# GpSimd adds the states of two pairs, and the order of all engines moves with it: residual and last attention group ahead of the convolution, whose second half uses another PSUM bank

## The reference

```
L0  whitening over 4 channel groups (means and a 4x4 covariance over all images), then a 4x4 mix and a bias
L1  per image: LayerNorm over channels, W_in -> xi, z (256 channels each); causal 4-tap convolution of xi, silu -> xc
    W_x: xc -> dt (8), B (16), C (16);  delta = softplus(W_dt dt + b)
    for n in 16 states:  h = h * exp(delta * A_n) + delta * xc * B_n      (a scan over the 1024 positions)
    y = sum_n h * C_n + xc * Dp;   y = y * silu(z);   out = W_out y + residual
L2  attention over the 1024 positions of an image (q, k, v, softmax), times gamma, plus its input
L3  a second attention (theta, phi, values = x), a 1x1 convolution, BatchNorm over all images, plus its input
```

## Time and profile before

| | |
|---|---|
| median of 3 runs | 5972.65 us (5970.45 to 5973.8) |
| profiled execution | 5973.68 us, its span 5971.9 us |
| PE busy | 5277.8 us (88%) |
| DVE busy | 5084.5 us (85%) |
| POOL busy | 3913.3 us (66%) |
| ACT busy | 3698.7 us (62%) |
| first scan, last scan start | 188.1 us, 5716.8 us |
| one round in the middle (copy into psU of k = 0 to the next one) | 2930.05 to 3106.84 us |

### The profile page before, as it was taken

One profiled execution on the slowest core, in us unless ns is written; L12 is line 12 of the kernel. 1 busy time (PEld: TensorE's weight loads), 2 busy tenths in 40 slices (PEclk: granted clock), 3 DMA queues, 4 the chain that ended last, 5 costly groups with the idle time before them and its releaser, 6 DMA issues.

```text
span 5971.9 us, 63803 instructions
## 1 busy us (share of the span) xinstructions
PE 5277.8 (88%) x18611; PEld 2975.7 (50%) x18611; DVE 5084.5 (85%) x5978; ACT 3698.7 (62%) x6077; POOL 3913.3 (66%) x2702
## 2 busy tenths in 40 slices
PE   6689999999999999999999999999999999999971
PEld 6245555545555555555555455555545555554541
DVE  5799888988988898988889888888888989888843
ACT  2566666666666666666666666666666666666643
POOL 0677766667766776767677776666766767767620
PEclk9799999999999999999999999999999999999996
DMA  3565555555555555555555555555555555555527
GB/s 125 204 229 206 206 206 198 207 207 205 207 207 205 204 210 205 211 201 212 205 196 211 213 205 201 205 207 196 211 212 204 208 205 207 202 205 212 199 106 285
DMA packets 199104, 1216.99 MB, mean 204 GB/s; under 512 B 27880, under 2 KB 28656, under 8 KB 67696
## 3 DMA queue, kind: packets, MB, share of 16 engines
q1 hardware_dynamic: 194416, 1196.26, 54.4%
q10 hardware_dynamic: 4352, 16.78, 0.7%
HBM read 1158.43 MB, written 54.53 MB: 203 GB/s over the span
## 4 chain that ended last, share of the span: by engine, by line
PE 38%; DVE 27%; ACT 19%; issue 13%; DMA 1%; POOL 1%; DVEq 1%; SPq 0%; ACTq 0%; POOLq 0%
PE psE L812 13%; PE psA L812 11%; DVE hs L486 11%; DVE psD L482 10%; PE psT L812 6%; ACT da L678 5%; ACT p L724 4%; PE psT L984 4%; DVE nm L511 3%; ACT pt L688 3%; PE psY L812 2%; ACT L647 1%; ACT L749 1%; ACT sz L650 1%; PE psD L812 1%
## 5 line engine op out<-in xcount | busy, mean ns | idle before, releaser
L301 POOL TENSOR_TENSOR pa<-hs,rows_all 128x1024 f32<-128x1024 f32 x1024 | 2410.4, 2354 | 1580.5 <-DVE hs L486 1577.8
L482 DVE TENSOR_TENSOR psD<-rows_all,psU 128x512 f32<-128x512 f32 x2048 | 1416.3, 692 | 70.2 <-POOL hlast L305 1.2
L678 ACT ACTIVATE da<-delta,neg_a 128x512 f32<-128x512 f32 x2048 | 1367.7, 717 | 119.4 <-DVE hs L486 108.7
L486 DVE TENSOR_TENSOR_SCAN hs<-da,hlast,psD 128x512 f32<-128x512 f32 x1024 | 1310.9, 1280 | 36.3
L486 DVE TENSOR_TENSOR_SCAN hs<-da,psD 128x512 f32<-128x512 f32 x1024 | 1248.9, 1220 | 36.1 <-ACT da L678 0.9
L812 PE MATMUL psY<-pa,ident 128*128 128x512 f32 x2304 | 1184.8, 610 | 50.7 <-POOL pa L308 30.5
L308 POOL TENSOR_TENSOR pa<-pa 128x512 f32<-128x512 f32 x896 | 1137.5, 1270 | 35.1
L724 ACT ACTIVATE p<-psE,nm 128x1024 f32<-128x1024 f32 x512 | 569.6, 1112 | 710.2 <-DVE nm L511 710.2
L812 PE MATMUL psA<-pt,va 128*128 128x256 f32 x4096 | 976.0, 387 | 2.6 <-DVE x L529 1.6
L812 PEld LDWEIGHTS psA<-pt,va 128*128 128x128 f32 x4096 | 794.8, 196 | 250.4 <-issue 153.9
L688 ACT ACTIVATE pt<-psT 128x512 f32<-128x512 f32 x1024 | 560.6, 597 | 451.6 <-PE psT L984 445.2
(11 more groups left out here) (180 smaller groups left out, 4564.7 us busy)
## 6 DMA issues: line engine op xcount, KB each, us to landing
rows_all<-bc_scratch SPq DMA_DIRECT2D x1024, 1024.0 KB, 4.7
xin<-x SPq DMA_DIRECT2D x40, 512.0 KB, 5.7
xres<-x SPq DMA_DIRECT2D x64, 256.0 KB, 4.2
x_scratch<-x SPq DMA_DIRECT2D x32, 512.0 KB, 2.9
f_scratch<-fa SPq DMA_DIRECT2D x32, 512.0 KB, 3.2
xres<-x SPq DMA_DIRECT2D x8, 512.0 KB, 3.2
x1g<-x SPq DMA_DIRECT2D x8, 512.0 KB, 3.3
fa<-x SPq DMA_DIRECT2D x8, 512.0 KB, 3.2
```

The costliest lines, as they stand in the source:

```text
L301: pool.tensor_tensor(pa[:, k % PROD, :, :], hs[:, sl, :, :], rows_all[:, slot, 2:4, :], ALU.mult).then_inc(S["prod"], 1)
L482: dve.tensor_tensor(psD[:, :], rows_all[:, slot, j, :], psU[:, :], ALU.mult).then_inc(S["dbu_ok"], 1)
L486: dve.tensor_tensor_scan(hs[:, sl, j, :], da[:, sl, j, :], psD[:, :], hlast[:, h, n_:n_ + 1] if ch else 0.0, ALU.mult, ALU.add).then_inc(S ...
L678: act.activation(da[:, k % 2, j, :], delta[:, h, cols(ch)], ACT.Exp, scale=neg_a[:, h, 2 * q + j:2 * q + j + 1]).then_inc(S["da_ok"], 1)
```

## The change

**GpSimd.** Every step now adds its two states (also 14 and 15), and every odd step then adds the slots of the two steps into one ("quad"). PE sums one slot for two steps: 8 matmuls a half. `prod`, `pair` and `quad` count POOL's stages; a slot comes free when PE has summed the quad (`quad_mm`).

**Order.** On PE the residual moves from line 3 to line 2, "weigh0 weigh1" of the last group stays in line 3, and the convolution follows: "inner0" from line 2 to 4, "inner1" from line 4 to 6. `normed` moves from step 2 to 3, the convolution's evictions on ACT from steps 3, 5 to 5, 7. Tile 1 is turned at step 10 (was 9); the groups are weighed one line later except the last, and `attended` moves from 12, 15 to 13, 16. "rows" moves ahead of the energy of tile 2, "steps" behind that of tile 3.

**Bank.** "inner1" goes to psA in place of psT's second bank and waits for the last attended group (`out_ok`); "project" waits only for the first half's eviction.

```
-ADDED = [r for r in range(16) if r not in (14, 15)]
...
-        TURN_AT = [8, 9, 12, 12, 14, 15, 17, 18]
+        TURN_AT = [8, 10, 12, 12, 14, 15, 17, 18]
...
-        WEIGH_AT = [(11, 11), (13, 14), (16, 17), (19, 19)]
-        ATTEND_AT = [12, 15, 18, 20]
+        WEIGH_AT = [(11, 12), (14, 15), (17, 18), (19, 19)]
+        ATTEND_AT = [13, 16, 18, 20]
...
-        AT_C, AT_N, AT_X, AT_Z, AT_B, AT_P = 0, 2, (3, 5), 9, 10, 11
+        AT_C, AT_N, AT_X, AT_Z, AT_B, AT_P = 0, 3, (5, 7), 9, 10, 11
...
-                    wait(pool, "pair_mm", b, k - PROD + 1)
+                    wait(pool, "quad_mm", b, k // 2 - 1)
...
-                    if k % NS in ADDED:
-                        wait(pool, "prod", b, k + 1)
...
+                    wait(pool, "prod", b, k + 1)
+                    pool.tensor_tensor(pa[:, k % PROD, 0, :], pa[:, k % PROD, 0, :], pa[:, k % PROD, 1, :], ALU.add
+                                       ).then_inc(S["pair"], 1)
+                    if k % 2:
+                        wait(pool, "pair", b, k + 1)
+                        pool.tensor_tensor(pa[:, k % PROD, 0, :], pa[:, (k - 1) % PROD, 0, :], pa[:, k % PROD, 0, :], ALU.add
+                                           ).then_inc(S["quad"], 1)
...
-                        act.activation(xc[:, h, cols(fc)], psT[:, h, :], ACT.Identity, bias=cbias[:, h, 0:1]
+                        act.activation(xc[:, h, cols(fc)], (psT[:, 0, :], psA[:, :])[h], ACT.Identity, bias=cbias[:, h, 0:1]
...
-                            wait(pe, "pt_ok", *att["turned1"])
+                            wait(pe, "pt_ok", *att["turned0"])
...
+                        dst = (psT[:, 0, :], psA[:, :])[h]
+                        if beside and h == 0:
                             wait(pe, "pt_ok", *beside["turned7"])
+                        if beside and h == 1:
+                            wait(pe, "out_ok", *beside["attended3"])
...
+                    if k % 2 == 0:
+                        return
+                    wait(pe, "quad", b, (k + 1) // 2)
+                    mm(psY[:, :], ident[:, :], pa[:, k % PROD, 0, :], start=(q == 1), stop=(q == PAIRS - 1)
+                       ).then_inc(S["quad_mm"], 1)
...
+                    if t == 1 and front:
+                        wait(pe, "z_ok", front[0], 2 * front[1] + 2)
...
-                    "turn add inner0",
-                    "weigh0 weigh1 residual add",
...
+                    "weigh1 turn add residual",
+                    "weigh0 weigh1 add",
```

More of the change, by code:

```diff
@@ L181, in build @@
             u_ok=2 * NCH, dbu_ok=2 * STEPS, da_ok=2 * STEPS, h_ok=2 * STEPS,
-            hlast_ok=STEPS // 2, prod=STEPS, added=NCH * len(ADDED), pair_mm=STEPS, g_ok=2 * NCH,
+            hlast_ok=STEPS // 2, prod=STEPS, pair=STEPS, quad=STEPS // 2, quad_mm=STEPS // 2, g_ok=2 * NCH,
             x1_mm=NCH, x1_ok=NCH, x1g_ok=NCH,
@@ L490, in gate @@
                 def gate(b, ch, h):
-                    wait(dve, "pair_mm", b, NS * ch + PAIRS * (h + 1))
+                    wait(dve, "quad_mm", b, (NS * ch + PAIRS * (h + 1)) // 2)
                     dve.tensor_tensor(g[:, h, cols(ch)], psY[:, :], sz[:, h, cols(ch)], ALU.mult
@@ L638, in front @@
                         h = AT_X.index(r)
-                        wait(act, "pair_mm", fb - 1, NS * (fc + 1))
+                        wait(act, "quad_mm", fb - 1, NS // 2 * (fc + 1))
                         wait(act, "xi_mm", fb, 2 * fc + h + 1)
-                        act.activation(xc[:, h, cols(fc)], psT[:, h, :], ACT.Identity, bias=cbias[:, h, 0:1]
+                        act.activation(xc[:, h, cols(fc)], (psT[:, 0, :], psA[:, :])[h], ACT.Identity, bias=cbias[:, h, 0:1]
                                        ).then_inc(S["xi_ok"], 1)
@@ L745, in image @@
                                 key(b - 1, c)
-                            if front_of and r == AT_X[1]:
+                            if front_of and r == AT_X[0]:
                                 front(*front_of, r)
@@ L757, in image @@
                                 value(b - 1, c)
-                            if front_of and r not in (AT_X[1], AT_Z):
+                            if front_of and r not in (AT_X[0], AT_Z):
                                 front(*front_of, r)
@@ L896, in front @@
                         wait(pe, "z_ok", fb, 2 * fc + 2)
+                        if att:
+                            wait(pe, "pt_ok", *att["turned1"])
                         for h in range(NH):
@@ L916, in front @@
                         wait(pe, "xc_ok", fb, 2 * fc + 2)
-                        if beside:
-                            wait(pe, "out_ok", *beside["attended3"])
+                        wait(pe, "xi_ok", fb, 2 * fc + 2)
                         for h in range(NH):
@@ L926, in sum_states @@
                     group, q = divmod(k, PAIRS)
-                    if q == 0:
+                    if q == 1:
                         wait(pe, "g_ok", b, group)
[L929 to L938, removed]
+                    if k % 2 == 0:
[3 more added lines that the diff above has]
+                       ).then_inc(S["quad_mm"], 1)
                 def skip_term(b, ch, h):
@@ L1016, in project @@
                     if front:
-                        wait(pe, "xi_ok", front[0], 2 * front[1] + 2)
-                    elif beside:
+                        wait(pe, "xi_ok", front[0], 2 * front[1] + 1)
+                    if beside:
                         wait(pe, "pt_ok", *beside["turned7"])
@@ L1033, in _ @@
                 ORDER = [
-                    "centre energy add weigh0 variance",
-                    "energy weigh1 turn add",
-                    "turn add inner0",
-                    "weigh0 weigh1 residual add",
-                    "inner1 add",
+                    "centre energy add variance",
+                    "energy turn add weigh0",
+                    "weigh1 turn add residual",
+                    "weigh0 weigh1 add",
+                    "inner0 add",
                     "project add",
-                    "add project_values",
+                    "project_values add inner1",
                     "energy add",
                     "energy turn add skip0",
[L1043 to L1049, removed]
+                    "gates add rows",
+                    "energy turn add",
+                    "energy steps add weigh0",
+                    "turn weigh1 turn_more skip1 add",
+                    "energy add",
+                    "energy turn weigh0 add",
+                    "turn weigh1 add",
                 ]
```

9 lines of the change are left out of this document (3 added, 6 removed).

## The result

| | before | changed |
|---|---|---|
| median | 5971.55 us (4 runs, 5969.71 to 5973.8) | 5763.54 us (4 runs, 5762.53 to 5769.15) |
| ratio to before | | 0.9653, 95% interval 0.9637 to 0.967 |

The change makes the kernel 3.5% faster, 208 us. Forecast was 5705 (267 less), in a range of 5600 to 5860.

A forecast was written before the change was run, and what follows sets the result against it. DVE's work and waits bound the kernel. Waits fall from 17.0 to 7.6 us a round, 291 over 31 rounds; round 0 adds 13, first halves 9: 5973.7 becomes 5705, range 5600 to 5860.

The forecast's parts named there:

- What bounds the kernel: DVE sets the pace: its work and its waits for psE tiles and rb; without waits a round lasts 159.8 us.
- Step 4: With PE's residual and last group ahead of the convolution, attended's wait of 4.1 us goes, with 2 us to spare.
- Together 17.0 us of 176.8: DVE's waits in one round before the change: 7.7 us for psE tiles plus 9.3 for rb.
- Step 12: The first group's attended moves a step later, so its wait of 0.4 us a half goes too.
- about 0.7: DVE's wait for tile 1 in a half, taken by the difference to 7.7/2 and expected to stay.
- Waits after: DVE's waits a half after the change: 0.7 + 1.0 + 1.3 + 0.8 = 3.8 us, 7.6 a round.
- hidden by 0.2: Tile 0 ready at 3056.6 where DVE wants it at 3056.8: just hidden, the first cover that can fail.
- a sign of being wrong: The forecast would be wrong if tile 0's maximum waits; two further signs concern POOL's waits and low clock.
- 0.8 for the clock: Added to tile 4's wait of 1.3 us in steps 11 to 13 for PE's half-clock stretches; bounds 0 and 3.4.
- POOL's 74.6 against 68: In round 0, without attention, POOL's 74.6 us a half exceeds DVE's 68 and becomes the bound: +13 us.
- Rival 1: PE idles more, energies 2 or 3 run at 1.2 GHz: 105 or 211 us more, 5810 to 5916; chance 0.18.
- Rival 3: xn is blocked for a whole GpSimd product: 1.65 us x 62 = 102 more, 5807; chance 0.03.

The follow-up runs named there:

- e3: The kernel before with PE's residual moved to the end of step 2 and inner0 behind the last attention group; 5674 us, ratio 0.9503.
- e12: The changed kernel plus 5 zero matmuls a half in PE's idle time, ahead of the energies of tiles 7 and 1; 5705 us, ratio 0.9553.
- e4: The changed kernel with the reciprocal of the second group's sums at step 13 in place of 12; 5766 us, ratio 0.9656.
- e7: The changed kernel plus ten zero matmuls a half ahead of the wait for the quad, giving PE 18 again; 5869 us, ratio 0.9823.
- e2: The changed kernel's order and bank, with GpSimd's products and sums as before, so PE has 18 adds a half; 5869 us, ratio 0.9829.
- e1: The kernel before with only GpSimd's sums of four states (quads), so PE has 8 adds a half; 6080 us, ratio 1.0182.
- e6: e1 plus ten zero matmuls a half ahead of the wait for the quad, giving PE 18 again; 5988 us, ratio 1.0019.
- e5: The changed kernel with tile 1 turned at step 9, rows behind tile 2's energy and steps ahead of tile 3's; 5687 us, ratio 0.951.
- e8: e3 (residual first) with GpSimd's sums of four states; 5704 us, ratio 0.9546, against the kernel before.
- e10: e5 plus 5 zero matmuls a half in PE's idle time, ahead of the energies of tiles 7 and 1; 5589 us, ratio 0.9366.
- e11: e8 plus 5 zero matmuls a half in PE's idle time, ahead of the energies of tiles 7 and 1; 5664 us, ratio 0.9486.

## Why the prediction was right, and where it was off

- **What bounds the kernel.** Right: DVE's work and its waits. 83.4 of a half less its 3.7 of waits is 79.7, as forecast (159.8 a round).
- **Step 4.** Right in mechanism and size: 4.2 a half before, nothing after, and e3 shows that this move alone carries more than the change. The 0.3 that is left for rb is another wait, which the walk passed over: the third group's `attended` stays at step 2 while the group is weighed a line later, and it waits 0.5 in first halves.
- **The sum's first term was mis-sized.** "Together 17.0 us of 176.8" was read from one round; the loop's mean is 14.6 of 174.3. The saving is 7.2 a round, not 9.4: 31 x 2.2 = 68 us, which by itself is more than the 58 by which the forecast missed. In that round tiles 3 and 4 and the first group's `attended` waited longer than in the mean (the 0.4 of "Step 12" is 0.1 in the mean), and tile 1's "about 0.7" was a difference: its rows in that round read 0.54 and 0.42.
- **Waits after.** Forecast 3.8 a half, measured 3.7, and that they agree is luck. The walk was made for a second half, and there the waits are 2.4; in a first half, for which it added 0.3, they are 5.1 (before, the two were alike, 7.4 and 7.3). By place, in the mean: tile 2 1.6 (forecast 1.0; second halves have 1.0, first halves 2.1, and e12 gives 1.1 without the low clock), tile 4 0.4 (2.1), tile 1 0 (0.7), tile 0 0.3 (hidden by 0.2, as it is in second halves; first halves wait 0.6, which the forecast had named as a sign of being wrong), and the reciprocal at step 12, 1.2, which the walk passed over. By the walk's own times tile 3's exponential ended at about 3087.3 (the evictions to 3086.2, then 1.1), and DVE stood at the reciprocal at about 3086.5, 3.1 behind the start of tile 3's maximum. e4 shows that the reciprocal's wait and tile 4's are one, 1.6 together, where 1.3 and 0.8 for the clock were forecast.
- **The clock.** e12 takes 0.8 a half of waits out, as much as the forecast's term for the clock, but at tile 2 and at the third group's rb, and mostly in first halves, not at tile 4.
- **POOL.** Right that it stays hidden in the loop (e7 against e2). Round 0 became 7.2 longer, from its first copy into psU to that of the next round (138.1 to 145.3), where 13 was forecast. The forecast set POOL's 74.6 against 68 in both halves; they went from 67.3 to 69.5 and from 70.9 to 75.8, with POOL busy for 65.6 and 73.0 us of them. So POOL is near its bound in both, but only the second has the work that was forecast for each.
- **Missed:** from the last copy into psU to the end it takes 304.5 us where it took 296.2, 8.3 more. Rounds 32 and 33 have no scan, and the chain of an attention is alone there. e2 (order alone) has 300.4 and e1 (quads alone) 295.6, so the order carries about half of it and the rest comes only with both. Which move of the order does it was not tested.
- **The pieces of the sum.** From the copy that starts round 1 to the last copy into psU the trace became 219.6 us shorter, where 282 were forecast (291 less the 9 for first halves); round 0 and the end add 7.2 and 8.3, where 13 was forecast. A slip that changes nothing: the lower end of the forecast's own range, without the clock's 0.8 and tile 1's 0.7, is 5705 - 62 x 1.5 = 5612 and not 5630.
- **Rival 1 (the clock)** had 0.18. In the changed kernel the clock is no lower than before (0.97 against 0.96; 4.9 us of a half at 1.2 GHz, 7.4 before), so it did not come about; but e1 with e6 shows its force: it is most of the 1.8% that the quads alone lose. My premise on PE's lost work, "By itself this is worth nothing where PE waits", was too kind: it can cost.
- **Rival 3 (xn blocked)** costs nothing here, with a mean of 1.3 against 1.4 before, but its mechanism is real, and the argument against it, that the longest was 1.449, does not hold for the changed kernel:

```profile
L468 DVE TENSOR_TENSOR xn<-xcen,rstd x64: 666/1353/2522, 162.1 to 5357.1; 128x512 f32<-128x512 f32 x64
```

The Trainium skill's page "SBUF — State Buffer", section "Who interferes with whom", has a VectorE instruction with two SBUF inputs and a GpSimd instruction that reads SBUF exclude each other. The traces agree. In the kernel before 63 of the 64 xn, and in the changed one 62, started while GpSimd had an add or a product running, and ended 0.54 to 0.57 us after its end; the others took 0.67 to 0.69. The longest of the changed kernel, xn (DVE) beside the product (POOL) that it waited for:

```profile
275.85 2.52 DVE L468 TENSOR_TENSOR xn<-xcen,rstd 128x512 f32<-128x512 f32 x1
...
275.48 2.35 POOL L300 TENSOR_TENSOR pa<-hs,rows_all 128x1024 f32<-128x1024 f32 x1
277.90 1.60 POOL L306 TENSOR_TENSOR pa<-pa 128x512 f32<-128x512 f32 x1
```

The product ends at 277.83, xn at 278.37, and the add behind it takes 1.60 in place of 1.27. So what xn costs hangs on the moment at which it starts, and every change of the order moves that.

What stays open: what the bank alone is worth (no run changes only that; e5 and e8, which share quads and residual first, differ by it, by the later convolution and by the groups a line later, and e5 is 18 us faster); why the second place, with tile 3's chain freed, does not pay more; and whether the clock's remaining low stretches behind rows and steps can be filled without delaying tile 3.

## What to carry to other kernels

Take the waits of a loop as means over its rounds, not from the round on the screen: here one round overstated them by 16%. Walk both halves of a round where they differ: a sum can come out right with both of them wrong. When several short in-order chains share an engine, put first what another engine waits for (the residual and the last group), and check each added wait of the reader behind every queue it passes, down to small instructions such as a reciprocal. And an engine that loses work may lose its clock: try the reduction alone, and if it does not pay, fill the idle time ahead of the critical matmuls.

## What the runs showed of the hardware

- Ten 128x512 matmuls a half less took TensorE's granted clock from 0.96 to 0.92 of 2.4 GHz (e1), and ten matmuls with a zero tile as weights brought it to 0.98 (e6), so matmuls that add nothing bring it back too.
- The same idle time goes with either clock. In the changed kernel tile 7's energy has 2.08 us of idle time ahead of it 61 times; 41 of these it took 1.98 or 1.99 us, and 20 of them 2.4 to 3.6:

```profile
589.07 1.98 PE L814 MATMUL psE<-ka,qa 128*128 128x512 f32 x4 [2.08 <-ACT p L726]
...
672.01 3.11 PE L814 MATMUL psE<-ka,x 128*128 128x512 f32 x4 [2.08 <-ACT p L726]
```

- Five zero matmuls a half in idle time, 4.3 us of work, gave 40 to 98 us on three orders (e10, e11, e12).
- xn, 128x512 with both inputs in SBUF, took 0.67 to 0.69 us with no GpSimd add or product running at its start, and otherwise until 0.54 to 0.57 us after the end of that one, up to 2.52 us.
